# A three-stage transformer kernel: the second stage's step pipeline is given other phases, other read orders and other block pairs

## What is computed

```python
ada = t_emb @ w_ada + b_ada
sh_msa, sc_msa, g_msa, sh_mlp, sc_mlp, g_mlp = jnp.split(ada, 6, axis=-1)
xn = layer_norm(logmap0(x))
xm = expmap0(xn * (1 + sc_msa) + sh_msa)
q, k, v = (_to_heads(plin(xm, w, b)) for w, b in ((w_q, b_q), (w_k, b_k), (w_v, b_v)))
attn = softmax(einsum('bhqd,bhkd->bhqk', logmap0(q), logmap0(k)) / 4)      # 16 heads of 16
out_h = expmap0(einsum('bhqk,bhkd->bhqd', attn, logmap0(v)))
attn_out = plin(_from_heads(out_h), w_o, b_o)
x = mobius_add(x, expmap0(g_msa * logmap0(attn_out)))
xm = expmap0(layer_norm(logmap0(x)) * (1 + sc_mlp) + sh_mlp)
ff = plin(plin(xm, w_f1, b_f1), w_f2, b_f2)                                # 256 -> 1024 -> 256
return mobius_add(x, expmap0(g_mlp * logmap0(ff)))
```

## Time and profile before

| | us |
|---|---|
| median of 3 runs | 3808.9 (3806.93 to 3816.92) |
| the profiled execution | 3806.83, its span 3804.7 |
| first stage, up to about 1215 | 1215 |
| ball block, run in of the pipeline, 1215 to 1297 | 82 |
| ball block, steps with attention, 1297 to 2150 | 853 |
| ball block, run out, 2150 to 2283 | 133 |
| third stage, from 2283 | 1522 |

### The profile page before, as it was taken

One profiled execution on the slowest core, in us unless ns is written; L12 is line 12 of the kernel. 1 busy time (PEld: TensorE's weight loads), 2 busy tenths in 40 slices (PEclk: granted clock), 3 DMA queues, 4 the chain that ended last, 5 costly groups with the idle time before them and its releaser, 6 DMA issues. The chain is left out here.

```text
span 3804.7 us, 51021 instructions
## 1 busy us (share of the span) xinstructions
PE 3407.3 (90%) x18088; PEld 1918.1 (50%) x18088; DVE 2125.5 (56%) x6120; ACT 1643.2 (43%) x3155; POOL 650.1 (17%) x266
## 2 busy tenths in 40 slices
PE   8999999999983587777788867999999999999998
PEld 3555555555551233433444444555555555555554
DVE  3334334334353345566556576777777777777773
ACT  2333333333331255444444424655555555555552
POOL 0000000000001544344433221111111111111110
PEclk9999999999996799889999988999999999999999
DMA  4010111011003000000000003000000000000000
GB/s 161 31 59 29 37 59 37 32 55 53 8 14 118 3 6 7 8 10 14 6 12 10 12 18 124 17 22 20 20 25 22 22 20 26 26 26 29 21 27 20
DMA packets 77550, 120.46 MB, mean 32 GB/s; under 512 B 10313, under 2 KB 66532, under 8 KB 72050
## 3 DMA queue, kind: packets, MB, share of 16 engines
q1 hardware_dynamic: 77298, 117.20, 9.0%
HBM read 96.16 MB, written 16.83 MB: 30 GB/s over the span
## 5 line engine op out<-in xcount | busy, mean ns | idle before, releaser
L2576 PE MATMUL wps<-w_wqkv,w_hT 128*128 128x512 f32 x768 | 378.4, 617 | 3.2 <-DMA w_wo<-in_wwo 3.2
L2198 POOL TENSOR_TENSOR w_rn<-w_n,w_mhalf 128x16 f32<-128x16 f32 x64 | 187.6, 2931 | 1096.5 <-DVE w_n L2376 1096.5
L2614 PE MATMUL wps<-w_xnT,w_w 128*128 128x512 f32 (+1 forms) x768 | 351.5, 598 | 24.5 <-DVE w_xnT L2439 20.3
L1267 POOL TENSOR_TENSOR bb_routh<-bb_rinh,b_expo 128x51 f32<-128x51 f32 x32 | 272.3, 8508 | 229.4 <-DVE bb_rinh L1478 229.4
L2226 ACT ACTIVATE w_pr<-w_sm,w_nmx,w_rn 128x256 f32<-128x256 f32 (+1 forms) x512 | 286.5, 562 | 10.0 <-DVE w_nmx L2357 9.4
L1298 ACT ACTIVATE bb_pr<-bb_ps 128x1024 f32<-128x1024 f32 x128 | 131.1, 1024 | 326.0 <-PE bb_ps L1806 325.5
L603 PE MATMUL ps<-xT,rw 128*128 128x512 f32 x512 | 245.5, 602 | 0.0
L2614 PEld LDWEIGHTS wps<-w_xnT,w_w 128*128 128x128 f32 (+1 forms) x768 | 133.2, 178 | 217.3 <-issue 193.7
L619 PE MATMUL ps<-hid,rw 128*128 128x512 f32 x512 | 240.7, 592 | 0.0
L2213 ACT ACTIVATE w_pT<-wps 128x512 f32<-128x512 f32 (+1 forms) x128 | 69.6, 544 | 329.5 <-PE wps L2523 329.5
L2576 PEld LDWEIGHTS wps<-w_wqkv,w_hT 128*128 128x128 f32 x768 | 137.8, 192 | 132.2 <-issue 127.1
(11 more groups left out here) (314 smaller groups left out, 6695.2 us busy)
## 6 DMA issues: line engine op xcount, KB each, us to landing
rw<-in_ew SPq DMA_DIRECT2D x32, 1024.0 KB, 6.8
w_xa<-xs SPq DMA_DIRECT2D x16, 512.0 KB, 3.9
w_xin<-xs SPq DMA_DIRECT2D x64, 128.0 KB, 3.8
xT<-in_xT SPq DMA_DIRECT2D x8, 512.0 KB, 3.6
xres<-in_x SPq DMA_DIRECT2D x32, 128.0 KB, 2.2
x<-x1t SPq DMA_DIRECT2D x32, 128.0 KB, 1.7
b_x<-x SPq DMA_DIRECT2D x1, 4096.0 KB, 14.2
bb_mod<-ada SPq DMA_DIRECT2D x16, 256.0 KB, 3.1
```

What stands on the lines that cost most here:

```text
L1267: g.tensor_tensor(routh[:], rinh[:], expo[:, 1, 0:HW], ALU.pow).then_inc(root_ok, 1)
L2198: g.tensor_tensor(rn[:, i % 2, t], n2[:, n % 2, 1], mhalf[:], ALU.pow).then_inc(nr_ok, 1)
L2576: ins = te.matmul(to, hT[:, i % 2, k, t * P:(t + 1) * P], wqkv[:, i // B, k, s * 512:(s + 1) * 512], start=(k == 0), stop=(k == KD - 1))
L2614: ins = te.matmul(to[0:n], w1[:, i // B, k, lo:lo + n], xnT[:, k], start=(k == 0), stop=(k == KD - 1))
```

## The change

The steps at which things are due are moved, and so is the order inside a step; nothing is computed otherwise, no tile is added.

- A tile's projections (both banks) are read by DVE in the step in which PE makes them (`projected` at a = 1 instead of 2), and PE makes the v part right behind q and k. `head_squares` moves from a = 3 to 2, `ask_heads` from 4 to 2, `limit_heads` from 6 to 5. So the power is asked one step after the product, and used three steps after it was asked instead of two.
- F1 is made in pairs: blocks (0, 1) at 37, (2, 3) at 39, (4, 5) at 41, (6, 7) at 43.
- The chain of a sequence moves to earlier steps: `step_limit` 21, `step_length` 22, `step_factors` 23, `applied` 24, `row_norms` 25, `row_angles` 26, `row_variances` 27, `row_scales` and `rows2` 28 and 29, `ask_rows2` 31, `limited_rows` 32, turning 33; second update `step_length` 53, `step_factors` 54, `result` 55 and 56.
- DVE's order in a step: `take`, `limit_heads`, `divide`, the first asks, `limit_hidden`, `output_rows`, `update` come first; then the chains; then `keys`, `rows`, `turned_rows2`, `hidden`; `projected`, `step_limit`, `ask_hidden`, `ask_heads` and `invert` last.
- POOL's order of roots follows DVE's new order of asking.

```diff
-            F1 = {37: (0,), 38: (1,), 39: (2, 3), 41: (4, 5), 42: (6, 7)}
+            F1 = {37: (0, 1), 39: (2, 3), 41: (4, 5), 43: (6, 7)}
...
                 if tile_due(G, 1) is not None:
                     yield "qk", tile_due(G, 1)
+                    yield "v", tile_due(G, 1)
...
-                if at(G, 35) is not None:
-                    yield "fu0", at(G, 35)
-                    yield "fu1", at(G, 35)
-                if tile_due(G, 1) is not None:
-                    yield "v", tile_due(G, 1)
+                if at(G, 33) is not None:
+                    yield "fu0", at(G, 33)
+                    yield "fu1", at(G, 33)
...
-                for kind, after in (("u", -23), ("m1", 21), ("m2", 22), ("r1", 27), ("r2", 30), ("u2", 33), ("n1", 51), ("n2", 52)):
+                for kind, after in (("m1", 21), ("n1", 51), ("u2", 31), ("r1", 25), ("r2", 27), ("n2", 52), ("u", -23), ("m2", 21), ("f", 45)):
                     if at(G, after) is not None:
                         yield kind, at(G, after)
-                if tile_due(G, 4) is not None:
-                    yield "h", tile_due(G, 4)
-                if at(G, 45) is not None:
-                    yield "f", at(G, 45)
+                if tile_due(G, 2) is not None:
+                    yield "h", tile_due(G, 2)
...
# ACT
-                    if tile_due(G, 3) is not None:
-                        head_squares(tile_due(G, 3))
+                    if tile_due(G, 2) is not None:
+                        head_squares(tile_due(G, 2))
...
# DVE
-                    if tile_due(G, 6) is not None:
-                        limit_heads(tile_due(G, 6))
-                    if tile_due(G, 2) is not None:
-                        projected(tile_due(G, 2))
+                    if tile_due(G, 5) is not None:
+                        limit_heads(tile_due(G, 5))
                     if group_due(G, 1) is not None:
                         divide(group_due(G, 1))
...
-                    if at(G, 31) is not None:
-                        row_scales(at(G, 31))
-                        rows2(at(G, 31), 0)
-                        rows2(at(G, 31), 1)
...
+                    if at(G, 24) is not None:
+                        applied(at(G, 24))
...
+                    if at(G, 28) is not None:
+                        row_scales(at(G, 28))
+                        rows2(at(G, 28), 0)
+                        rows2(at(G, 28), 1)
...
+                    if at(G, 56) is not None:
+                        result(at(G, 56), 1)
...
                     if among(G, F1):
                         for m in among(G, F1)[1]:
                             hidden(among(G, F1)[0], m)
-                    if tile_due(G, 4) is not None:
-                        ask_heads(tile_due(G, 4))
+                    if tile_due(G, 1) is not None:
+                        projected(tile_due(G, 1))
+                    if at(G, 21) is not None:
+                        step_limit(at(G, 21), "m1", "m2")
                     if at(G, 45) is not None:
                         ask_hidden(at(G, 45))
+                    if tile_due(G, 2) is not None:
+                        ask_heads(tile_due(G, 2))
                     if group_due(G, 0) is not None:
                         invert(group_due(G, 0))
```

More of the change, by code:

```diff
@@ L1194, in squares_due @@
                 for p in range(2):
-                    if at(G, 31 + p) is not None:
+                    if at(G, 28 + p) is not None:
                         for t in (2 * p, 2 * p + 1):
-                            yield "u2", at(G, 31 + p), t
+                            yield "u2", at(G, 28 + p), t
                 if among(G, YS):
@@ L1249, in _ @@
                         gates2(b + 1)
-                    b = at(G, 59)
+                    b = at(G, 56)
                     if b is not None:
@@ L1746, in _ @@
                         ask("n1", at(G, 51), YA2[:, at(G, 51) * NT:at(G, 51) * NT + NT], EPS * EPS)
+                    if at(G, 31) is not None:
+                        ask_rows2(at(G, 31))
+                    if at(G, 46) is not None:
+                        limit_hidden(at(G, 46))
+                    if among(G, YS):
+                        output_rows(*among(G, YS))
+                    for p in range(2):
+                        if at(G, 19 + p) is not None:
+                            update(at(G, 19 + p), p)
@@ new lines, in _ @@
+                    if at(G, 22) is not None:
+                        step_length(at(G, 22), "m2", th1_ask)
+                    if at(G, 23) is not None:
+                        step_factors(at(G, 23), th1_ok)
+                    if at(G, 24) is not None:
+                        applied(at(G, 24))
+                    if at(G, 25) is not None:
+                        row_norms(at(G, 25))
+                    if at(G, 26) is not None:
+                        row_angles(at(G, 26))
+                    if at(G, 27) is not None:
+                        row_variances(at(G, 27))
@@ L1747, in _ @@
+                    if at(G, 28) is not None:
+                        row_scales(at(G, 28))
+                        rows2(at(G, 28), 0)
+                        rows2(at(G, 28), 1)
+                    if at(G, 29) is not None:
+                        rows2(at(G, 29), 2)
+                        rows2(at(G, 29), 3)
+                    if at(G, 32) is not None:
+                        limited_rows(at(G, 32))
                     if at(G, 52) is not None:
                         step_limit(at(G, 52), "n1", "n2")
+                    if at(G, 53) is not None:
+                        step_length(at(G, 53), "n2", th2_ask)
@@ L1749, in _ @@
                     if at(G, 54) is not None:
-                        step_length(at(G, 54), "n2", th2_ask)
+                        step_factors(at(G, 54), th2_ok)
                     if at(G, 55) is not None:
-                        step_factors(at(G, 55), th2_ok)
+                        result(at(G, 55), 0)
                     if at(G, 56) is not None:
-                        result(at(G, 56), 0)
-                    if at(G, 59) is not None:
-                        result(at(G, 59), 1)
+                        result(at(G, 56), 1)
@@ L1757, in _ @@
+                    if at(G, -23) is not None:
+                        ask_rows(at(G, -23))
                     if at(G, -21) is not None:
@@ L1760, in _ @@
                         keys(tile_due(G, 7))
-                    for p in range(2):
-                        if at(G, 19 + p) is not None:
-                            update(at(G, 19 + p), p)
                     if rows_due(G):
                         rows(*rows_due(G))
-                    if at(G, 35) is not None:
-                        turned_rows2(at(G, 35))
+                    if at(G, 33) is not None:
+                        turned_rows2(at(G, 33))
                     if among(G, F1):
@@ L1908, in _ @@
                         heads(tile_due(G, 1), "qk", 0, 2 * D)
+                        heads(tile_due(G, 1), "v", 2 * D, 3 * D)
                     if group_due(G, 1) is not None:
@@ L1914, in _ @@
                         turn_rows(tile_due(G, 0))
-                    if at(G, 35) is not None:
-                        turn_rows2(at(G, 35))
-                    if tile_due(G, 1) is not None:
-                        heads(tile_due(G, 1), "v", 2 * D, 3 * D)
+                    if at(G, 33) is not None:
+                        turn_rows2(at(G, 33))
                     if group_due(G, 0) is not None:
```

28 lines of the change are left out of this document (11 added, 17 removed).

## The result

Over four runs the changed kernel takes 3745.55 us (3741.54 to 3749.14) against 3809.02 (3806.93 to 3816.92): a ratio of 0.9829, 95% interval 0.9812 to 0.9847. It is 63 us faster. The forecast was 3725, in a range of 3660 to 3785.

A forecast was written before the change was run, and what follows sets the result against it. PE's idle time, mostly the spread's 106.8 us wait for `projected`, was taken as the bound. Light steps -19.0, transition -24.4, steady periods -33.9, steps 101 to 109 -0.4 and -2.9, run-in -1.5, run-out -1: total -83, 3725 us, range 3660 to 3785.

The forecast's parts named there:

- A: Steady period from the spread of step 1 to that of 5, PE's own content: 26.2 us, 6.0 less.
- B: Steady period from the spread of step 5 to that of 9, DVE's sum of work: 31.4 us, 2.4 more.
- The term for the adds: Steps 5 to 9: POOL's adds hold up DVE about 1.0 us each; 0 to 4 us, taken as 2.9.
- C: Steady period from the spread of step 9 to that of 13, a chain through POOL: 26.4 us, 4.2 less.
- D: Steady period, spread of step 13 to 1: PE's 25.5 plus `invert` and slow clock; 27.9 us, 3.5 less.
- Light parts: Attention steps before the spread of step 33, head loop binds: 15.9 us per four steps, now 21.4; together -19.0.
- The transition: From the spread of step 33 to that of 53: -5.7, -2.5, -3.1, -4.4, -8.7, together -24.4 us.
- Run-out: After step 109 and run-out: one chain of norms whose length stays, same operations; -1 us, bounds -10 and +8.
- PE binding everywhere: Rival: all waits of the spread go, each period takes 94 to 98 us; 3655 us, chance 0.12.
- The renamed wait: Rival: DVE ends steps 8 and 12 later, two period parts cost 4 to 5 us more each; 3780, chance 0.17.
- The slower case: Rival: ACT waits at `hidden_squares` of steps 7 and 11 for POOL's adds behind the head power; 3826 us, chance 0.07.
- The change doesn't do what it says: Rival of no change: waits pass one for one from `projected` to `invert`, light parts too; 3809 us, chance 0.06.

The follow-up runs named there:

- the experiment: Changed kernel with POOL's adds of blocks cut from 512 to 8 columns (output is another): 3682.03 us.
- the kernel with `rows2` later: Changed kernel with `rows2` one step later (29 and 30 instead of 28 and 29): 3723.31 us.
- the kernel with the head phases alone: Kernel before with only the change's steps for `projected`, `head_squares`, `ask_heads`, `limit_heads` and the v part: 3843.7 us, ratio 1.0085.
- the halves: Kernel before with nothing but the new head phases: 3843.7 us, ratio 1.0085; changed kernel with the old head phases: 3840.57 us, ratio 1.0077.
- the same kind of move: Changed kernel, second update's `step_factors` at 58, `result` at 59 and 60: 3750.05 us; `applied` at 25, atop later `rows2` and last sequence's old chain steps: 3706.63 us.

## Why the forecast was nearly right, and where it missed

**The bound and the mechanism** held. The wait for `projected` is gone, the one for `invert`'s copy took its place, and the part of the period where each wait stands is the one named: 4.23 us in step 9, 3.75 in step 13, 0.16 or none in steps 1 and 5. Step 9's was forecast at 7 to 8 us, and this did not follow from the forecast's own terms: 31.4 less PE's 20.7 leaves 10.7. The trace has 4.23 before the spread, 2.25 before the second projection, which waited for a bank that `hidden` frees, and some 3.3 by which the four groups behind that (1720.56 to 1727.7, granted clock 0.50) are longer than elsewhere. The part's length does not depend on how this is split, since DVE's sum sets it.

**A, forecast 26.2, measured 26.0.** The turning job and the output projection wait for nothing.

**B, 31.4 and 30.8.** DVE shows no gap of 0.7 us from 1703 to 1731.9: it is DVE's sum. The term for the adds, 2.9 with bounds 0 and 4, measured 2.97 on the operations with block 0's copy, 2.67 without it and 2.7 by the experiment. The term for the power, nothing, held as well: without it B is 31.0.

**C, 26.4 and 27.9.** The chain is the one described (power 8.5, two adds, root, two adds, `rows2`), and POOL shows it:

```profile
1741.16 8.50 POOL L1264 TENSOR_TENSOR bb_routh<-bb_rinh,b_expo 128x51 f32<-128x51 f32 x1 [2.76 <-DVE bb_rinh L1475]
1749.62 2.67 POOL L1278 TENSOR_TENSOR bb_acc<-bb_acc,bb_fsq 128x512 f32<-128x512 f32 x2
1752.26 1.02 POOL L1267 TENSOR_TENSOR bb_routs<-bb_rins,b_expo 128x4 f32<-128x4 f32 x1
1753.25 2.78 POOL L1278 TENSOR_TENSOR bb_acc<-bb_acc,bb_fsq 128x512 f32<-128x512 f32 x2
```

The power starts 9.2 us after the spread, not 7.7. The mis-sized term is the pair of F1 blocks: 6.13 us at the slow clock after the new wait of step 9, where I had taken the 4.71 of the earlier trace rows. `ask_heads` stands behind their two `hidden`. (The terms listed for C add up to 26.25; the forecast has 26.4.)

**D, 27.9 and 27.9**, with F2 at 5.16 after the 3.75 us wait. The period: 112.6 against 111.9. That the three periods together came within 0.5 us (-34.4 for -33.9) is part luck: they gained 13.5, 10.6 and 10.3 us, where I had 11.3 for each.

**Light parts, 3.7 us short.** Six of the seven came within 1.0 us: 16.9, 16.3 and 16.5 where I had 15.9 each, 21.5 for 22.1, 20.5 for 20.4, 17.8 for 17.7. The one from step 25 measured 21.2 for 19.1. There the logarithm of the row angles stands on ACT right in front of the next exponentials:

```profile
1426.91 1.28 ACT L1378 ACT_TABLE_LOAD   x1
1428.21 0.21 ACT L1378 ACTIVATE b_cols<-b_cols 128x4 f32<-128x4 f32 x1
1428.43 1.28 ACT L1295 ACT_TABLE_LOAD   x1
1429.73 1.02 ACT L1295 ACTIVATE bb_pr<-bb_ps 128x1024 f32<-128x1024 f32 x1
```

```profile
1431.72 2.09 PE L1803 MATMUL bb_ps<-bb_qT,bb_kT 32*128 32x512 f32 x8 [2.75 <-ACT bb_pr L1296]
```

2.8 us stand in front of the exponentials, PE's scores wait 2.75 for them and run at the slow clock. My step named only POOL's chain there and left ACT's queue out. The transition missed by 2.0, nearly all of it in the parts from step 41 (27.3 for 26.4) and 45 (29.4 for 27.8).

**Run-out, the largest miss.** "One chain of norms whose length stays: -1, bounds -10 and +8" measured +11.8, and +14 with the steps from 109 on, outside my bounds, and past the 10 that I had named as a sign of being wrong. The step that failed is the claim that the same operations take the same time. They do not stand where they stood: with the chain two or three steps earlier it shares DVE's queue with the copies of F1 blocks that PE is waiting for. In the kernel with `rows2` later, putting the chain back returned 7.4 of 15.7 us; the cause of the other 8 stays open. Beside it the run-in gained 3 us more than forecast, and the stages the change doesn't touch differ by 7.2 between the two executions.

**The rivals.** PE binding everywhere did not happen (101.4 us busy in 112.7). The renamed wait did happen, with half the total, but not at the sizes of that rival. The slower case shows in part C, where ACT stands 2.40 and 0.78 us in `hidden_squares` for POOL's adds, and PE's scores wait 0.23 us for the exponentials behind them. The 18.5 us of late exponentials here, against 12.9 before, lie mostly outside the steady periods. In the kernel with the head phases alone it came true: 6.06 us in part C, 41.0 in all. (In the rival with PE binding, 150 us off the profiled execution make 3657 and not 3655.) "The change doesn't do what it says" is excluded.

What I had not seen at all is that the change is one thing and not a list. I priced each part against before and added; measured alone, the halves have the opposite sign. The forecast of the parts came out because it was made by following each engine's queue in the final order, not by the list of edits.

## What to carry to other kernels

On an engine that works in order, what a long operation costs is what stands behind it: look for every short request behind the 8.5 us one before moving either, since the order of two requests was worth some 34 us. Cut a period at one recurring instruction, sum each engine's queue in each part in the final order, and do the same for the run-out with the copies and chains that fall together there. Work moved off the binding part pays only where it lands in slack: the same kind of move was worth 0 and 8 us.

## What the runs showed of the hardware

POOL's adds of 512 columns (1.27 us each) hold DVE's operations up, on SBUF operands of 48 to 256 columns, one-input forms too: 0.88 for 0.18, 1.19 for 0.21, and 2.17 for a pair that takes 1.18 when the adds have 8 columns. The 8.5 us power on 51 columns held up nothing that the rows show: in the changed kernel both `step_factors` and the first scalings lie inside it at their usual lengths. The Trainium skill ("SBUF — State Buffer", Who interferes with whom) has one rule for both, an exclusive lock for the whole instruction; the adds agree with it in kind and the power does not.

PE's granted clock is lowered after the idle stretches of 4.23 and 3.75 us: 0.58 of full speed from 1733.0 to 1738.9 and 0.71 from 1762.3 to 1767.4, that is at the 1.2 GHz level for most of it, and 1.00 in the same products later (1744.4 to 1748.0, 1776.2 to 1779.8). The F1 pair took 6.13 there and F2 5.16, against 3.60 and 3.62. It was also lowered behind the 2.25 us of idle before 1720.56: 0.50 from 1721 to 1727, 1.00 before. After 0.40 us of idle in the kernel with `rows2` later the clock stayed at 1.00. The price does not follow the length of the wait: in that kernel 5.51 us of idle in step 9 were followed by an F1 pair of 5.32. One such wait thus costs twice, and what is behind it in PE's order pays the second time: taking the 3.75 us away gave 6.8 in C and D, 0.8 of it by that shorter F1 pair.
